# Moving five weight maxima and two patch normalisations between the steps of a fused vision-text layer

## The chip, the cores and the metric

The kernel runs on one core of a Trainium2 chip, as one program that holds the whole layer. The metric is the device time of one execution in microseconds. Three executions of the kernel before took 753.91, 754.61 and 766.34 us; the median is 754.61.

## The reference

64 images of 3 x 96 x 96 are cut into 36 patches of 768 numbers each. The patches are normalised, projected to 256 numbers, normalised again; a class token is put ahead and 32 text tokens behind, which gives 64 sequences of 69 tokens. Then come attention with 16 heads and rotary positions, and a layer of 8 experts, two for each token.

```python
patches = x.reshape(b, C, h, P, w, P).transpose(0, 2, 4, 3, 5, 1).reshape(b, h * w, P * P * C)
z = _layernorm(patches, ln1_g, ln1_b)
z = jnp.einsum('bnp,pe->bne', z, W_proj) + b_proj
z = _layernorm(z, ln2_g, ln2_b)
z = jnp.concatenate([cls, z], axis=1)
z = z + pos_emb
...
h = jnp.concatenate([h, txt], axis=1)
h = h + _L0_attn_ref(_layernorm(h, axis=-1), wq, wk, wv)
h = h + _L0_ffn_ref(_layernorm(h, axis=-1), moe_router, moe_w13, moe_w2)
```

## The kernel before

**Tiles.** The 2,304 patches make 18 patch tiles of 128 rows (n = 0 to 17), the 4,416 tokens make 35 token tiles (g = 0 to 34), and attention runs over 64 sequences (b). The work up to the experts is written as steps t from -12 (START) on. Each engine has a function `step(t)` that lists, under conditions on t, what the engine does in that step, and runs it for t = -12, -11 and so on. So the order on each engine is written out by hand, and engines meet only through semaphores; an engine that waits holds everything behind it in its own order. Steps aren't synchronised: engines can be some steps apart.

**Patch tiles.** Tiles 0 to 5 (EARLY) have their projection at the steps -10 to -5. One step later VectorE takes the statistics of z (`st2`, `mv2`) and PoolE (GpSimd) makes `rs2` and `off2`; two steps later ScalarE normalises z into `zout` (L1328) and PoolE multiplies by the gain and adds the positions (L819, L821); three steps later SyncE (SP) stores zout to the DRAM tensor `h_rows`, in four or five pieces (L637). `off2` and `rs2` have one buffer: PoolE makes those of tile n only when tile n - 1 is normalised (`zn_ready`). zout has two: ScalarE normalises tile n only when tile n - 2 is stored. Tiles from 6 on have their projection at the steps 4, 8, 13, 17 and so on.

**Token tiles.** SP loads a tile of tokens back as `h` (L613), VectorE takes its statistics (L1161, L1164), PoolE makes `off3`, ScalarE writes `xn` (L1367), PE turns it (L1460), ScalarE rounds it to fp16 as `fx_hi` (L1289), VectorE takes the rest as `fx_lo` (L1138), PE projects q and k (L1467), VectorE multiplies by the rotary table (`rot`, L1147), adds up k (L1153) and PoolE q (L784), PE turns both, and ScalarE saves `qT`, `kE`, `kO`. These take one step each: loads at first[g] - 6 and projection at first[g] - 2, for g = 0, 1, 2 and so on at the steps -2, -1, 1, 3, 5, 7, 9, 10, 12 and 14 (PJ). The other steps from 0 to 14 have no projection.

**Attention.** For sequence b, at step b PE makes the scores (L1607) in the PSUM tensor `quad`, and VectorE reduces them to row maxima (`nm_src`, L1101). At step b + 2 PE makes the scores again, turned, with the maxima taken off (L1671, L1675), again in quad, and ScalarE takes the exponentials (`probs`, L1383), for which the next scores in quad wait; at b + 3 PE weighs the values (L1575). So in each step scores, reduction, second scores and exponentials follow each other.

**Weight maxima.** The expert weights are later kept in fp16 halves under one common scale, which is found from their largest absolute value. For that SP loads them in 24 parts of 128 x 1024 (512 KB, L671) into a ring of three buffers `w_part`, and VectorE reduces each part to one column of `largest` (L1207). Part n is reduced at step -9 + n, one a step, to step 14, and its load is issued two steps before. The reduction stands near the end of VectorE's step: behind the statistics, and ahead of the next step's reduction of scores. At step 15 VectorE takes the maximum over all parts; the weights themselves are split from step 17 on.

## Time and profile before

| | |
|---|---|
| median of three runs | 754.61 us |
| the profiled execution | 758.35 us |
| its span, first to last instruction | 756.6 us |
| PE busy | 695.0 us (92%) |
| DVE (VectorE) busy | 549.4 us (73%) |
| POOL (GpSimd) busy | 456.1 us (60%) |
| ACT (ScalarE) busy | 403.6 us (53%) |
| mean granted TensorE clock | 0.951 |

The span is what one profiled execution took from its first to its last instruction. A busy share is an average over stages that have different limits. The page cuts the span into 40 slices of 18.9 us; the row of the granted clock (in tenths of full speed) shows where PE was given less:

```profile
PE   7857999999999999998888999999999999999994
DVE  3778887888888888897994457888756666566662
PEclk9977999999999999996995899999999999999999
```

The steps that the change touches run from about 30 to 142 us, in the slices 2 to 8. The experts begin at about 417 us.

### The profile page before, as it was taken

To read this page: it belongs to the slowest core of one execution; us is meant where nothing else is said; L and a number is where in the kernel's file an instruction comes from. 1 tells how busy PE (TensorE), PEld (TensorE's weight loads), DVE (VectorE), ACT (ScalarE), POOL (GpSimd) and SP (SyncE) were. 2 spreads that over 40 slices of the span, in tenths; PEclk is the share of its full clock that TensorE was granted. 3 is DMA by queue.
4 is the path that set the end of the run, shared out by engine and by line. 5 is a ranking of instruction groups with operands and counts; after the bars stand their busy time and mean duration, and the time that the engine had idled before them with its cause. 6 is when DMAs were issued, how large, how long until landed. Compare 5 with 4: busy or idle time off the path is not lost. (4 is left out here: it accounts for less than half of the span.)

```text
span 756.6 us, 27578 instructions
## 1 busy us (share of the span) xinstructions
PE 695.0 (92%) x9680; PEld 479.2 (63%) x9680; DVE 549.4 (73%) x1171; ACT 403.6 (53%) x893; POOL 456.1 (60%) x634
## 2 busy tenths in 40 slices
PE   7857999999999999998888999999999999999994
PEld 6724666767677776766667565556666666656663
DVE  3778887888888888897994457888756666566662
ACT  3334666677788778775765443333444434444341
POOL 5573644556576665645655367778666666666654
PEclk9977999999999999996995899999999999999999
DMA  8578666455545555553532377876878687777764
GB/s 296 183 212 288 206 197 219 128 154 169 167 138 176 152 176 141 169 155 110 139 113 83 96 121 127 107 122 114 128 128 134 121 140 124 131 135 127 134 113 77
DMA packets 145434, 112.52 MB, mean 149 GB/s; under 512 B 93545, under 2 KB 126073, under 8 KB 145240
## 3 DMA queue, kind: packets, MB, share of 16 engines
q1 hardware_dynamic: 129927, 86.75, 43.7%
q0 software_dynamic: 15376, 24.01, 19.1%
q8 instruction: 85, 1.39, 0.8%
q14 instruction: 46, 0.37, 0.2%
HBM read 58.95 MB, written 24.90 MB: 111 GB/s over the span
## 5 line engine op out<-in xcount | busy, mean ns | idle before, releaser
L425 POOL DMA_INDIRECT out<-qk,token_of x76 | 124.7, 1641 | 88.6 <-DVE small L513 47.5
L526 PE MATMUL quad<-w_hi,fx_hi 128*128 x304 | 116.2, 382 | 0.5 <-ACT fx_hi L453 0.5
L526 PE MATMUL quad<-w_lo,fx_hi 128*128 x304 | 116.2, 382 | 0.0
L526 PE MATMUL quad<-w_hi,fx_lo 128*128 x304 | 116.2, 382 | 0.0
L526 PE MATMUL bank<-w_hi,v 128*128 x608 | 112.0, 273 | 2.7 <-DMA v<-kO 2.3
L1383 ACT ACTIVATE probs<-quad 69x1104 f32<-69x1104 f32 x64 | 69.6, 1088 | 60.0 <-PE quad L1675 59.9
L1101 DVE TENSOR_REDUCE nm_src<-quad 69x16 f32<-69x1104 f32 x64 | 82.8, 1294 | 25.6 <-PE quad L1607 25.5
L490 DVE SCALAR_TENSOR_TENSOR probs<-quad,up_scale,vb 128x512 f32<-128x512 f32 x76 | 56.8, 748 | 52.1 <-PE quad L526 51.4
L402 POOL DMA_INDIRECT wc<-xn_rows,token_of x72 | 73.6, 1023 | 23.9 <-issue 19.6
L461 ACT ACTIVATE vb<-quad,unscale 128x512 f32<-128x512 f32 x76 | 52.3, 688 | 59.0 <-PE quad L526 58.9
L526 PE MATMUL bank<-w_lo,v 128*128 x304 | 82.9, 273 | 0.0
L526 PEld LDWEIGHTS bank<-w_hi,v 128*128 128x128 f16 x608 | 59.6, 98 | 18.3 <-issue 4.7
L736 POOL TENSOR_TENSOR rs<-ve,eps_pow 128x1 f32<-128x1 f32 (+1 forms) x106 | 62.3, 588 | 8.8
L784 POOL TENSOR_TENSOR qk<-rot 128x256 f32<-128x256 f32 (+1 forms) x35 | 34.0, 970 | 52.8 <-DVE rot L1147 52.8
L735 POOL TENSOR_SCALAR ve<-mv 128x1 f32<-128x1 f32 (+1 forms) x106 | 29.9, 282 | 57.7 <-DVE mv L1164 24.2
L776 POOL TENSOR_TENSOR h<-hb,att 128x256 f32<-128x256 f32 (+1 forms) x35 | 35.3, 1007 | 42.7 <-issue 30.7
L469 ACT ACTIVATE kE<-probs 128x512 f16<-128x512 f32 x38 | 24.0, 631 | 63.5 <-DVE probs L490 63.5
L469 ACT ACTIVATE kO<-probs 128x512 f16<-128x512 f32 x38 | 23.9, 630 | 63.0 <-DVE probs L490 63.0
L1671 PE MATMUL quad<-qT,kE 32*69 32x69 f32 x1024 | 46.8, 253 | 10.2 <-DVE nm_src L1101 9.9
L1467 PE MATMUL bank<-wqkv_hi,fx_hi 128*128 128x512 f16 (+2 forms) x140 | 49.8, 356 | 6.2 <-DVE fx_lo L1138 3.5
L526 PEld LDWEIGHTS quad<-w_hi,fx_lo 128*128 128x128 f16 x304 | 29.9, 98 | 35.8 <-issue 1.0
L1675 PE MATMUL quad<-nm,sel 32*69 32x69 bf16 x1024 | 51.6, 197 | 0.0
(273 smaller groups left out, 1768.3 us busy)
## 6 DMA issues: line engine op xcount, KB each, us to landing
w_lo<-in_experts_w SPq DMA_DIRECT2D x24, 512.0 KB, 6.3
w_raw<-in_experts_w SPq DMA_DIRECT2D x48, 256.0 KB, 4.2
xt<-in_patches SPq DMA_DIRECT2D x18, 384.0 KB, 6.0
h<-h_rows SPq DMA_DIRECT2D x34, 128.0 KB, 5.4
hb<-h_rows SPq DMA_DIRECT2D x34, 128.0 KB, 4.8
out<-h SPq DMA_DIRECT2D x34, 128.0 KB, 4.6
xn_rows<-xn SPq DMA_DIRECT2D x34, 128.0 KB
vb<-v SPq DMA_DIRECT2D x30, 138.0 KB
```

What stands on the lines that cost most here:

```text
L402: nc.gpsimd.indirect_dma_start(xg[n % DEPTH], None, reach(xn_rows, n), bass.IndirectOffsetOnAxis(token_of[:, n:n + 1], 0)).then_inc(gather ...
L425: nc.gpsimd.indirect_dma_start(reach(out, n), bass.IndirectOffsetOnAxis(token_of[:, n:n + 1], 0), y[q], None, compute_op=ALU.add).then_inc ...
L461: nc.scalar.activation(silu[q], quad[:, 2 * q, :], ACT.Silu, scale=unscale[:, 1:2]).then_inc(d["silu_ready"], 1)
L469: nc.scalar.activation(hid_parts[q][:, 0, :], hid[q], ACT.Copy).then_inc(d["hid_hi_ready"], 1)
L490: nc.vector.scalar_tensor_tensor(out=hid[q], in0=quad[:, 2 * q + 1, :], scalar=up_scale[:, :], in1=silu[q], op0=ALU.mult, op1=ALU.mult).th ...
L526: last = nc.tensor.matmul(dst, x[:, k, :], w[:, bass.ds(col + k * (2 * width if width == HIDDEN else width), width)], start=(k == 0 and m ...
L736: nc.gpsimd.tensor_tensor(rs, ve, eps_pow[0:rs.shape[0], :], ALU.pow).then_inc(signal, 1)
L1101: nc.vector.tensor_reduce(nm_src[b % 2][:, :].rearrange("p (g j) -> p g j", g=4)[:, :, 0:4], quad[0:SEQ, :, 0:4 * SEQ].rearrange("p g (j k ...
L1383: nc.scalar.activation(probs[b % 2][0:SEQ, :, :], quad[0:SEQ, :, 0:4 * SEQ], ACT.Exp, scale=HEAD_DIM ** -0.5).then_inc(s["probs_ready"], 1)
L1467: to = nc.tensor.matmul(dst, x[g % 2][:, k, 0:r], w[:, k, cols], start=(k == 0 and m == 0), stop=(k == KD - 1 and m == 2))
L1671: nc.tensor.matmul(quad[0:SEQ, g, j * SEQ:(j + 1) * SEQ], (kE, kO)[odd][band, c, at:at + SEQ], qT[band, c, at:at + SEQ], start=True, stop= ...
L1675: to = nc.tensor.matmul(quad[0:SEQ, g, j * SEQ:(j + 1) * SEQ], sel[band, j, :], nm[b % 2][band, :], start=False, stop=True)
```

## The change

The table of steps at which a part is reduced, so far one a step from -9 to 14, becomes a written list, `PART_STEPS`. The steps -6, -4, -1, 0 and 1 no longer have a part, and the steps 4, 6, 8, 11 and 13, none of which has a projection, have two. The load of a part is issued two steps ahead of its reduction, or, where its buffer comes free later than that, one step behind the reduction of the part three places before. And the patch tiles 4 and 5 (`LATE_NORM`; the fifth and the sixth) are normalised three steps behind their projection, not two: at -3 and -2 on ScalarE and PoolE, and their stores on SP come at -2 and -1. The semaphores and what they count stay as they are.

```diff
-PART_FROM = 3
+PART_STEPS = [-9, -8, -7, -5, -3, -2, *range(2, 15), 4, 6, 8, 11, 13]
+LATE_NORM = (4, 5)
...
-                part_step = {START + PART_FROM + n: n for n in range(PARTS)}
-                SCALE_STEP = START + PART_FROM + PARTS
+                part_step, part_load, part_at = {}, {}, sorted(PART_STEPS)
+                for n, k in enumerate(part_at):
+                    part_step.setdefault(k, []).append(n)
+                    part_load.setdefault(max(k - 2, part_at[n - PART_BUFS] + 1 if n >= PART_BUFS else k - 2), []).append(n)
+                SCALE_STEP = part_at[-1] + 1
+                normed = {mm_step[n] + (3 if n in LATE_NORM else 2): n for n in range(NT)}
...
-                            behind = t in HL and t - 3 in ZM and last_patch_tile[HL[t]] >= ZM[t - 3]
+                            behind = t in HL and t - 1 in normed and last_patch_tile[HL[t]] >= normed[t - 1]
...
-                            if t - 3 in ZM:
-                                n = ZM[t - 3]
+                            if t - 1 in normed:
+                                n = normed[t - 1]
...
-                            if t + 2 in part_step:
-                                n = part_step[t + 2]
+                            for n in part_load.get(t, ()):
...
-                            if t - 2 in ZM:
-                                n = ZM[t - 2]
+                            if t in normed:
+                                n = normed[t]
...
-                            if t in part_step:
-                                n = part_step[t]
+                            for n in part_step.get(t, ()):
```

The pieces with `t - 2 in ZM` stand twice, on PoolE and on ScalarE. Line numbers of the changed kernel are 5 or 6 higher from the planner on.

On ScalarE, from step -4 (xn of token tile 0) to step -1 (qT), before:

```order
L1367 ACTIVATE xn<-h,off,rs 128x256
L1328 ACTIVATE zout<-z,off,rs 128x256
L1289 ACTIVATE fx_hi<-bank 128x256
L1367 ACTIVATE xn<-h,off,rs 128x256
L1328 ACTIVATE zout<-z,off,rs 128x256
L1289 ACTIVATE fx_hi<-bank 128x256
L1289 ACTIVATE v<-bank,unscale 128x16x16
L1289 ACTIVATE qT<-bank 128x2x128
```

And now:

```order
L1372 ACTIVATE xn<-h,off,rs 128x256
L1294 ACTIVATE fx_hi<-bank 128x256
L1372 ACTIVATE xn<-h,off,rs 128x256
L1333 ACTIVATE zout<-z,off,rs 128x256
L1294 ACTIVATE fx_hi<-bank 128x256
L1294 ACTIVATE v<-bank,unscale 128x16x16
L1333 ACTIVATE zout<-z,off,rs 128x256
L1294 ACTIVATE qT<-bank 128x2x128
```

The first zout (patch tile 4) went behind fx_hi of token tile 0 and xn of token tile 1, the second (patch tile 5) behind fx_hi of tile 1 and v of tile 0.

On PoolE, at the steps -4 (the last off) to -1 (the second qk), before:

```order
L740 TENSOR_SCALAR off<-mv,rs 128x1
L819 TENSOR_TENSOR zout<-zout,gain 128x256
L821 TENSOR_TENSOR zout<-zout,shift 128x256
L819 TENSOR_TENSOR zout<-zout,gain 128x256
L821 TENSOR_TENSOR zout<-zout,shift 128x256
L784 TENSOR_TENSOR qk<-rot 128x256
L735 TENSOR_SCALAR ve<-mv 128x1
L736 TENSOR_TENSOR rs<-ve,eps_pow 128x1
L740 TENSOR_SCALAR off<-mv,rs 128x1
L784 TENSOR_TENSOR qk<-rot 128x256
```

And now:

```order
L746 TENSOR_SCALAR off<-mv,rs 128x1
L825 TENSOR_TENSOR zout<-zout,gain 128x256
L827 TENSOR_TENSOR zout<-zout,shift 128x256
L790 TENSOR_TENSOR qk<-rot 128x256
L741 TENSOR_SCALAR ve<-mv 128x1
L742 TENSOR_TENSOR rs<-ve,eps_pow 128x1
L746 TENSOR_SCALAR off<-mv,rs 128x1
L825 TENSOR_TENSOR zout<-zout,gain 128x256
L827 TENSOR_TENSOR zout<-zout,shift 128x256
L790 TENSOR_TENSOR qk<-rot 128x256
```

The pair of patch tile 5 went behind the addition of q of token tile 0 and the small chain of token tile 2.

On VectorE, from k of token tile 1 at step -1 to the score reduction of step 2, before:

```order
L1153 TENSOR_TENSOR qk<-rot 128x256
L1207 TENSOR_REDUCE largest<-w_lo 128x1
L1101 TENSOR_REDUCE nm_src<-quad 69x4x4
L1138 TENSOR_TENSOR fx_lo<-bank,fx_hi 128x256
L1161 BN_STATS st<-h 128x6
L1164 BN_AGGR mv<-st 128x2
L1207 TENSOR_REDUCE largest<-w_lo 128x1
L1101 TENSOR_REDUCE nm_src<-quad 69x4x4
L1147 TENSOR_TENSOR rot<-bank,rope_sb 128x1024
L1153 TENSOR_TENSOR qk<-rot 128x256
L1207 TENSOR_REDUCE largest<-w_lo 128x1
L1101 TENSOR_REDUCE nm_src<-quad 69x4x4
```

And now:

```order
L1159 TENSOR_TENSOR qk<-rot 128x256
L1107 TENSOR_REDUCE nm_src<-quad 69x4x4
L1144 TENSOR_TENSOR fx_lo<-bank,fx_hi 128x256
L1167 BN_STATS st<-h 128x6
L1170 BN_AGGR mv<-st 128x2
L1107 TENSOR_REDUCE nm_src<-quad 69x4x4
L1153 TENSOR_TENSOR rot<-bank,rope_sb 128x1024
L1159 TENSOR_TENSOR qk<-rot 128x256
L1107 TENSOR_REDUCE nm_src<-quad 69x4x4
```

The maxima ahead of the score reductions of steps 0, 1 and 2 are gone (they stood at the steps -1, 0 and 1). At step 4 and in the same way at 6, 8, 11 and 13 the row of the maximum now reads `x2`, in its old place.

## Rows read from the trace of the kernel before

**Rows 1.** The page: busy time, share of the span and instructions of each engine.

```profile
PE 695.0 (92%) x9680; PEld 479.2 (63%) x9680; DVE 549.4 (73%) x1171; ACT 403.6 (53%) x893; POOL 456.1 (60%) x634
```

**Rows 2.** Windows: busy us (count) PE, PEld, DVE, ACT, POOL; PEclk, DMA, GB/s.

```profile
60.00:80.00 20.00, 17.58 (x292) 11.38 (x293) 16.82 (x26) 9.37 (x25) 7.84 (x16) 0.74 0.76 251
80.00:150.00 70.00, 64.52 (x1442) 47.25 (x1442) 58.01 (x104) 44.54 (x109) 37.23 (x78) 0.95 0.61 188
```

**Rows 3.** Timeline, steps -4 and -3: start us, us, engine, line, operation, idle before.

```profile
43.47 0.66 PE L1460 MATMUL bank<-idt,xn 128*128 128x128 f32 x2 [3.67 <-ACT xn L1367]
...
44.74 0.60 ACT L1328 ACTIVATE zout<-z,off,rs 128x256 f32<-128x256 f32 x1 [1.41 <-DMA h_rows<-zout]
...
45.05 1.19 DVE L1207 TENSOR_REDUCE largest<-w_lo 128x1 f32<-128x1024 f32 x1
45.24 0.36 ACT L1289 ACTIVATE fx_hi<-bank 128x256 f16<-128x256 f32 x1
...
46.16 0.41 DVE L1138 TENSOR_TENSOR fx_lo<-bank,fx_hi 128x256 f16<-128x256 f32 x1
...
46.72 0.59 PE L1467 MATMUL bank<-wqkv_hi,fx_hi 128*128 128x512 f16 x1 [2.59 <-DVE fx_lo L1138]
...
46.86 0.60 ACT L1367 ACTIVATE xn<-h,off,rs 128x256 f32<-128x256 f32 x1 [1.26 <-POOL off L740]
46.91 0.22 POOL L735 TENSOR_SCALAR ve<-mv 128x1 f32<-128x1 f32 x1
...
48.91 0.73 POOL L821 TENSOR_TENSOR zout<-zout,shift 128x256 f32<-128x256 f32 x1
```

**Rows 4.** Timeline, steps -2 to 1.

```profile
51.95 0.96 POOL L784 TENSOR_TENSOR qk<-rot 128x256 f32<-128x256 f32 x1 [0.82 <-DVE rot L1147]
...
57.35 0.96 POOL L784 TENSOR_TENSOR qk<-rot 128x256 f32<-128x256 f32 x1 [3.11 <-DVE rot L1147]
57.64 1.21 DVE L1207 TENSOR_REDUCE largest<-w_lo 128x1 f32<-128x1024 f32 x1
...
58.77 1.29 DVE L1101 TENSOR_REDUCE nm_src<-quad 69x16 f32<-69x1104 f32 x1
...
60.31 0.23 PE L1607 MATMUL quad<-kE,qT 32*69 32x69 bf16 x4 [1.30 <-ACT kO L1289]
```

**Rows 5.** Timeline, steps 1 to 3.

```profile
64.99 1.21 DVE L1207 TENSOR_REDUCE largest<-w_lo 128x1 f32<-128x1024 f32 x1
...
66.12 1.29 DVE L1101 TENSOR_REDUCE nm_src<-quad 69x16 f32<-69x1104 f32 x1
...
67.47 0.52 PE L1671 MATMUL quad<-qT,kE 32*69 32x69 f32 x8 [1.10 <-DVE nm_src L1101]
...
69.00 0.43 DVE L1161 BATCH_NORM_STATS2 st<-h 128x6 f32<-128x256 f32 x1 [1.26 <-DMA h<-h_rows]
```

**Rows 6.** Timeline of DVE (one row of PE), steps 4 to 14.

```profile
81.41 0.48 DVE L1090 SCALAR_TENSOR_TENSOR z<-bank,rs,bias 128x256 f32<-128x256 f32 x1 [0.54 <-PE bank L1681]
82.52 1.30 DVE L1101 TENSOR_REDUCE nm_src<-quad 69x16 f32<-69x1104 f32 x1 [0.62 <-PE quad L1607]
...
92.45 1.30 DVE L1101 TENSOR_REDUCE nm_src<-quad 69x16 f32<-69x1104 f32 x1 [0.89 <-PE quad L1607]
...
103.89 0.48 DVE L1090 SCALAR_TENSOR_TENSOR z<-bank,rs,bias 128x256 f32<-128x256 f32 x1 [0.55 <-PE bank L1681]
105.40 1.30 DVE L1101 TENSOR_REDUCE nm_src<-quad 69x16 f32<-69x1104 f32 x1 [1.02 <-PE quad L1607]
...
120.08 0.32 PE L1575 MATMUL bank<-probs,vb 69*32 69x69 f32 x8 [1.64 <-issue]
...
121.51 1.30 DVE L1101 TENSOR_REDUCE nm_src<-quad 69x16 f32<-69x1104 f32 x1 [1.75 <-PE quad L1607]
...
133.22 0.48 DVE L1090 SCALAR_TENSOR_TENSOR z<-bank,rs,bias 128x256 f32<-128x256 f32 x1 [0.21 <-PE bank L1681]
134.34 1.30 DVE L1101 TENSOR_REDUCE nm_src<-quad 69x16 f32<-69x1104 f32 x1 [0.63 <-PE quad L1607]
```

## Predicting the time

> **What bounds the kernel now.** I read the page first: the span is 756.6 us, PE is busy 695.0 us of it, and no other engine comes near [rows 1]. That share hides what matters here. The windows view shows the granted clock. In the stretch from 60 to 80 us it averages 0.74, from 80 to 150 us it averages 0.95, and VectorE is busy 16.82 of 20 us in the first [rows 2]. The clock has two levels, 1.2 and 2.4 GHz (0.50 and 1.00), so 0.74 means that (1 - 0.74) / 0.5 = 52% of those 20 us, 10.4 us, ran at half speed. So in the first steps of the attention loop PE is often a waiting engine, slow once it gets going. Then I read the timeline of all engines from 43 to 71 us and the VectorE timeline on to 135 us.
>
> At steps -4 and -3 the first projection starts late. PE has turned token tile 0 from 43.47 (its record is 0.66 long), but ScalarE is held in the normalisation of patch tile 4 (44.74, after 1.41 us of waiting for the stores that free its buffer) and evacuates fx_hi only at 45.24. VectorE runs a maximum at 45.05 and makes fx_lo at 46.16; the projection begins at 46.72 [rows 3]. At steps -1 and 0 the maximum at 57.64 stands ahead of the score reduction at 58.77; the next scores start at 60.31 and name ScalarE's kO as what came last [rows 4]. At steps 1 and 2 the maximum at 64.99 stands ahead of the reduction at 66.12, and PE's second score pass (L1671) waits 1.10 us for that reduction and starts at 67.47 [rows 5]. Behind 142 us nothing that the change touches is left, and the chain runs in order through the same instructions; what is gained or lost there I carry to the end one for one.
>
> **The change, part by part.** No instruction is added or taken away: 24 loads of 512 KB and 24 maxima stay. A maximum costs VectorE 1.10 to 1.13 us from its start to the next start (45.05 to 46.16, 64.99 to 66.12) [rows 3, 5]; I use 1.1.
>
> *Step -6.* Its maximum goes. Behind it the next work is the statistics of h tile 0, which waits for a load anyway, and then PoolE work; I take 0, with 0 and 1.1 as bounds.
>
> *Step -4 and the later normalisation of tile 4.* ScalarE can take fx_hi when PE's turn ends, 43.47 + 0.66 = 44.13, instead of 45.24. It is then done by 44.5, and VectorE, without the maximum at 45.05, takes fx_lo at 45.05 instead of 46.16: 1.1 us. Both edits are needed: with the maximum gone alone fx_lo would wait for fx_hi until 45.6 (0.55 gained), with the normalisation moved alone the maximum would hold it (0 gained). The projection begins at 45.6. What the move puts at risk is PoolE: at step -4 it computes the offset of tile 5 only once tile 4 is normalised, and that now stands in ScalarE's step -3, behind xn of tile 1 (46.86 to 47.46). ScalarE ends it at 48.06; PoolE then has to do what it does now from 46.91 to 48.91 + 0.73, 2.7 us, and with a start-up of 0.3 comes to the addition of q at about 51.05, where it stood at 51.95 [rows 3, 4]. The rotation that it needs would be there at about 50.8, so of 1.1 us 0.9 survives. The second zout pair (tile 5) moves behind that addition, into a wait of PoolE of 3.1 us ahead of the next one [rows 4]: 0. The stores of tiles 4 and 5 come a step later too, five DMA issues of some 2 us in all on SP's queue at step -1, ahead of the first two loads of vb and of h tile 4; vb is wanted three steps later. I count 0 and keep this as a rival. Term: 0.9 (bounds 0 and 1.1).
>
> *Steps -1 and 0.* Without the maximum at 57.64 the reduction at 58.77 starts 1.1 us sooner on top of the 0.9. But the next scores, at 60.31, came when ScalarE's kO of tile 1 was there, and that hangs on the projection, which moved by 0.9 only [rows 4]. So these two maxima were hidden behind PE and ScalarE: 0 (bounds 0 and 2.2).
>
> *Step 1.* The maximum at 64.99 goes, the reduction starts 1.1 us sooner, and PE's pass at 67.47 and the exponentials and scores behind it with it: PE waited 1.10 us for just this [rows 5]. Term: 1.1 (bounds 0 and 1.1).
>
> *The doubled steps 4, 6, 8, 11 and 13.* The second maximum takes 1.1 us of VectorE and costs only what it exceeds the idle time between the first one and the next score reduction [rows 6]. Step 4: VectorE is idle 0.54 ahead of z (81.41) and 0.62 ahead of the reduction at 82.52, 1.16 in all: 0. Step 6: 0.89 ahead of 92.45: 0.2. Step 8: 0.55 ahead of z and 1.02 ahead of 105.40: 0. Step 11: 1.75 ahead of 121.51: 0; most of that cover is a hole of 1.64 us in PE's own stream (120.08, "issue"), without which the step would cost the full 1.0. Step 13: 0.21 ahead of z and 0.63 ahead of 134.34: 0.3. Together 0.5 (bounds 0 and 5.5).
>
> *The sum*: 0.9 + 1.1 - 0.5 = 1.5 us gained. The profiled execution took 758.35 us (span 756.6) and would take 756.85; the median of the runs is 754.61, so I forecast 754.6 - 1.5 = **753.1 us**. The profiled execution lies 3.7 us over the median, more than twice the effect, so a change of this size is near the least that the runs can show.
>
> **The clock.** The row of 60 to 80 us says that 10.4 us ran at half speed, and PE was busy 17.58 us of that stretch, so dense but slow [rows 2]. If the waits that go leave PE denser and a third of that time comes back at full speed, 10.4 / 3 / 2 = 1.7 us more are gained; at the utmost 5.2. In the other direction, the stretch from 80 to 150 us has 0.05 / 0.5 = 10% or 7.0 us at half speed; another 3.5 us of it would cost 1.7. The Trainium skill, "TensorE: Matmul & The Clock Gate", section "HAM oscillation — how this bites in real kernels", says that bursts of matmuls broken by waits fall back to the slow clock again and again. By that rule the gain would be 3.2 us rather than 1.5, at the price just worked out. It cuts both ways: by the same rule the five doubled steps, where PE now runs at full clock, might lose it. The trace agrees so far as the slow stretches all lie behind waits of PE, but it cannot say where they fall after the change.
>
> **The rivals.**
> - *The doubled maxima are not covered (slower).* VectorE is the bound of the steps without a projection as soon as the idle time behind a maximum is under 1.1 us. Rows 6 show 1.16, 0.89, 1.57, 1.75 and 0.84; four of the five are near that point [rows 6], and a step that PE reaches sooner (a warmer clock, no hole at 120.08) loses its cover. Price: 5 x 1.1 - 2.0 = 3.5 us, 758.1 us. Against it: all five waits are for PE, whose program is the same, and it has nothing that would bring it sooner by itself.
> - *Nothing arrives.* The projections at half clock and the waits for h bound the steps, and what is won at -4 and 1 is only waited for later: VectorE waits 1.26 us for h at 69.00 already [rows 5]. 754.6 us.
> - *The clock comes back as well*: 1.5 + 1.7 to 1.5 + 3.4, so 751.4 to 749.7, say 750.5 us. For it: slow stretches just behind the waits that go; and three loads of 512 KB fewer in steps -3 to -1 also bring h sooner.
> - *The clock is lost later*: 753.1 + 1.7 = 754.8 us.
> - *SP's queue*: the late stores delay h of tile 4, whose wait of 1.26 grows by as much again: 753.1 + 1.3 = 754.4 us [rows 5].
>
> **How the numbers follow.** Forecast (751.6 to 754.2): 0.45. Clock back: 0.20. Nothing arrives: 0.14. Maxima not covered: 0.12. Clock lost: 0.05. SP's queue: 0.04. The range that leaves out no more than 2 in 10 goes from 748.8, where the sum and the full 3.4 us of clock come together and a little of the rest of the 5.2, to 757.5, where nearly all five maxima are exposed; the likeliest case alone is 751.6 to 754.2. Faster or slower by over 2% is 15 us, about what a measurement of this kernel can tell from no change, and no case reaches it: faster 0.01, same 0.97, slower 0.02.
>
> **What would show it.** In the profile after: fx_lo of tile 0 near 45.1 and the projection near 45.6; q added near 51; the first reduction near 56.8 with no maximum ahead of it; the scores of step 1 still waiting for kO, at 59.4; PE's pass of step 2 near 65.4 with no wait for VectorE. Then the reductions of steps 5, 7, 9, 12 and 14 1.5 to 2 us sooner than now, which says that the doubled maxima were free; if this lead shrinks by 1 us at one of them, that one was not. A first projection that is not sooner, or PoolE's addition of q no sooner than 51.95, would show the term of step -4 wrong; a mean clock in 58 to 76 us unlike 0.74 would show the rival.

## The result, and the profile after

Six runs of the changed kernel took 766.04 to 775.34 us, median 769.79; six runs of the kernel before beside them had a median of 757.12. The ratio is 1.017, with a 95% interval of 1.013 to 1.022: the change makes the kernel some 13 us slower. Ratios here and below leave out executions that fell in a slower state, whatever the kernel (766.34 us once here, 1316.53 and 1651.04 us once each below); the medians hold them. I had forecast 753.1 us, 1.5 less than the median of three runs before (754.61), and at most 757.5. Direction and range were wrong.

The page of the profiled execution (775.34 us, the longest of the six), instructions by engine and three rows of the 40 slices (19.3 us each here):

```profile
PE 699.0 (90%) x9680; PEld 482.4 (62%) x9680; DVE 551.1 (71%) x1171; ACT 403.5 (52%) x893; POOL 455.9 (59%) x634
...
PE   7864998799999999998888999999999999999994
...
DVE  4765888678978878987996466788755665666562
...
PEclk9968889899999999997895799999999999999997
```

The counts are those of [rows 1] and the busy times within 4 us of them, while the span grew by 17.0 (756.6 to 773.6). So the new time is waiting. The windows, with the columns of [rows 2]:

```profile
58.00:64.00 6.00, 3.76 (x51) 2.26 (x51) 5.13 (x8) 3.19 (x8) 2.05 (x5) 1.00 0.54 151
64.00:76.00 12.00, 4.01 (x78) 2.42 (x78) 3.75 (x6) 3.17 (x7) 2.48 (x6) 0.81 0.70 230
76.00:80.00 4.00, 3.84 (x86) 3.23 (x87) 3.90 (x7) 1.61 (x3) 2.06 (x5) 0.50 0.75 238
80.00:150.00 70.00, 60.13 (x1258) 43.30 (x1259) 56.19 (x89) 38.12 (x92) 30.09 (x62) 0.89 0.68 215
```

From 64 to 76 us PE works 4.01 us of 12, and no other engine more than 3.75; behind it PE runs at half clock for 4 us (0.50). To place the losses I compared the starts of the 64 score reductions (`nm_src`), one for each step, in the timelines of both kernels. After minus before, in us:

| step | 0 | 1 | 2 | 3 | 5 | 8 | 12 | 13 | 14 | 16 | 40 | 63 |
|---|---|---|---|---|---|---|---|---|---|---|---|---|
| changed kernel | -1.4 | -1.7 | -2.8 | +4.0 | +4.6 | +5.8 | +6.8 | +5.8 | +10.5 | +12.8 | +12.9 | +13.8 |

A lead of 2.8 us is built up to step 2; step 3 loses 6.8, and the steps 14 to 16 lose 7.0. The remaining 3.2 us of the span come behind the last reduction. These sizes are those of one execution, and the longest of six: the places of the losses are firmer than their sizes.

**The lead** has the forecast's sign, but not its terms. Timeline from step -4 on; each line is a start, a duration, an engine, a line, an operation, and the idle time before it:

```profile
44.08 0.38 ACT L1294 ACTIVATE fx_hi<-bank 128x256 f16<-128x256 f32 x1 [0.59 <-PE bank L1465]
44.49 0.42 DVE L1144 TENSOR_TENSOR fx_lo<-bank,fx_hi 128x256 f16<-128x256 f32 x1
...
45.06 0.58 PE L1472 MATMUL bank<-wqkv_hi,fx_hi 128*128 128x512 f16 x1 [1.02 <-DVE fx_lo L1144]
...
50.98 0.91 POOL L790 TENSOR_TENSOR qk<-rot 128x256 f32<-128x256 f32 x1
...
57.41 1.30 DVE L1107 TENSOR_REDUCE nm_src<-quad 69x16 f32<-69x1104 f32 x1
...
59.92 0.23 PE L1612 MATMUL quad<-kE,qT 32*69 32x69 bf16 x4 [1.29 <-ACT kO L1294]
...
60.30 1.30 DVE L1107 TENSOR_REDUCE nm_src<-quad 69x16 f32<-69x1104 f32 x1 [0.71 <-PE quad L1612]
61.70 1.22 DVE L1153 TENSOR_TENSOR rot<-bank,rope_sb 128x1024 f32<-128x1024 f32 x1
...
63.30 1.30 DVE L1107 TENSOR_REDUCE nm_src<-quad 69x16 f32<-69x1104 f32 x1
...
64.65 0.36 PE L1676 MATMUL quad<-qT,kE 32*69 32x69 f32 x8
```

And before, between the scores of step 1 (60.31 [rows 4]) and their reduction:

```profile
60.86 1.19 DVE L1207 TENSOR_REDUCE largest<-w_lo 128x1 f32<-128x1024 f32 x1
61.96 1.29 DVE L1101 TENSOR_REDUCE nm_src<-quad 69x16 f32<-69x1104 f32 x1
```

PoolE's q comes 0.97 us sooner, the scores of step 1 only 0.39 us (PE's turn of q and k took 1.11 us instead of 0.66). Their reduction comes 1.66 us sooner, since the maximum of step 0 no longer stands ahead of it, and that of step 2 comes 2.82 us sooner without the maximum of step 1. So the lead is about 0.4 + 1.3 + 1.1 us, and nearly half of it is the maximum of step 0.

**The first loss** stands right behind it:

```profile
73.14 0.43 DVE L1167 BATCH_NORM_STATS2 st<-h 128x6 f32<-128x256 f32 x1 [8.22 <-DMA h<-h_rows]
...
76.16 0.52 PE L1676 MATMUL quad<-qT,kE 32*69 32x69 f32 x8 [7.28 <-DVE nm_src L1107]
```

VectorE waits 8.22 us for token tile 4, where it waited 1.26 [rows 5]. The statistics stand ahead of the reduction of step 3 on VectorE, and PE waits 7.28 us for that. SP's own queue in that stretch (here the duration is that of the issue alone):

```profile
55.56 1.87 SPq L644 DMA_DIRECT2D h_rows<-zout  x5
57.48 1.54 SPq L663 DMA_DIRECT2D vb<-v  x2
59.06 0.78 SPq L665 DMA_DIRECT2D vb<-v  x1
59.89 0.48 SPq L677 DMA_DIRECT2D w_lo<-in_experts_w  x1
60.95 0.34 SPq L620 DMA_DIRECT2D h<-h_rows  x1
```

The load was issued at 60.95, only 0.9 us later than before (60.01), but took 12.2 us to land (60.95 to 73.14) instead of 9.0 (60.01 to 69.00). So it isn't SP's queue that is slow, but what the load meets once it is issued. The five late stores now stand directly ahead of the first loads of `vb`.

**The second loss**, VectorE and SP at the steps 11 to 14:

```profile
126.97 1.22 DVE L1212 TENSOR_REDUCE largest<-w_lo 128x1 f32<-128x1024 f32 x1 [0.97 <-DMA w_lo<-in_experts_w]
...
133.34 1.97 SPq L677 DMA_DIRECT2D w_lo<-in_experts_w  x2
...
141.77 1.22 DVE L1212 TENSOR_REDUCE largest<-w_lo 128x1 f32<-128x1024 f32 x1 [4.04 <-DMA w_lo<-in_experts_w]
143.34 1.22 DVE L1212 TENSOR_REDUCE largest<-w_lo 128x1 f32<-128x1024 f32 x1 [0.35 <-DMA w_lo<-in_experts_w]
```

Both parts of step 13 are issued in SP's step 12, one step ahead and not two: with three buffers their places in the ring come free only with the two reductions of step 11. The same holds for the steps 6 and 8, and by the rule of the diff single parts lose a step as well (those of 5, 7, 9, 10, 12 and 14): 14 of the 24 loads go out one step ahead. VectorE then waits 4.04 + 0.35 us for the two of step 13. The other 2.6 us up to step 16 have no wait for a part beside them; PE's granted clock from 145 to 150 us is 0.51, where it was 1.00 before.

### The profile page after: what moved, and what is told of

It reads as the page before. It is cut to its first block and busy times, and to the rows that moved or that the text cites. A ratio compares the mean times of both kernels' runs of the same rounds, so it can differ in the third digit from the quotient of the medians.

```text
span 773.6 us, 27578 instructions
## 1 busy us (share of the span) xinstructions
PE 699.0 (90%) x9680; PEld 482.4 (62%) x9680; DVE 551.1 (71%) x1171; ACT 403.5 (52%) x893; POOL 455.9 (59%) x634
## 5 line engine op out<-in xcount | busy, mean ns | idle before, releaser
L497 DVE SCALAR_TENSOR_TENSOR probs<-quad,up_scale,vb 128x512 f32<-128x512 f32 x76 | 56.8, 748 | 54.8 <-PE quad L533 54.3
L741 POOL TENSOR_SCALAR ve<-mv 128x1 f32<-128x1 f32 (+1 forms) x106 | 28.2, 266 | 66.4 <-DVE mv L1170 31.8
L1676 PEld LDWEIGHTS quad<-qT,kE 32*69 32x69 f32 x1024 | 30.3, 148 | 40.2 <-DVE nm_src L1107 27.0
```

The source lines that it names most:

```text
L497: nc.vector.scalar_tensor_tensor(out=hid[q], in0=quad[:, 2 * q + 1, :], scalar=up_scale[:, :], in1=silu[q], op0=ALU.mult, op1=ALU.mult).th ...
L1676: nc.tensor.matmul(quad[0:SEQ, g, j * SEQ:(j + 1) * SEQ], (kE, kO)[odd][band, c, at:at + SEQ], qT[band, c, at:at + SEQ], start=True, stop= ...
```

## The experiments

Three theories to begin with. *S*: the later normalisation, by its stores, delays h at step 3. *L*: the loads of doubled parts, with one step of lead, are late. *D*: the doubled maxima themselves cost VectorE's time. All ratios below are to runs of the kernel before on the same chip, in three rounds unless said otherwise, with 95% intervals. Its median was 759.83 us beside the first four kernels, and 758.64 (order, even cut, table with four buffers), 756.52 (odd cut to the kernel before with the cut), 759.01 and 759.23 us beside the later groups. The ratios aren't quotients of these medians. The two differ most in the group at 756.52, where the executions of before lie in two heaps (754 to 759 and 760 to 765 us): the quotients for its four kernels are 1.018, 1.014, 1.008 and 1.004 where the ratios given below are 1.0096, 1.0097, 1.0033 and 0.9981. No reading below rests on that difference. "Lead" is the start of a score reduction against the profiled execution of before, minus being sooner. A single lead is rough: in two kernels that differ from before up to step 1 in nothing or only in the pieces of vb (*doubled maxima* and *before, cut* below), the reduction of step 1 starts 0.6 and 2.3 us later than there.

### Each part of the change alone

The later normalisation alone, and the table alone:

```diff
-PART_STEPS = [-9, -8, -7, -5, -3, -2, *range(2, 15), 4, 6, 8, 11, 13]
+PART_STEPS = list(range(-9, 15))
```

> The parts stand as before (one a step, -9 to 14); only the normalisations of patch tiles 4 and 5 come one step later. Theory S (the late stores of tile 5 push the first vb load on SP from 55.05 to 57.48, and its rows and those of the second vb share few DMA engines with the load of h tile 4, whose wait at VectorE grows from 1.26 to 8.2 us): most of the loss at steps 2 to 3 appears here, 755 + 4 to 6 us, and VectorE waits over 5 us for h. Theory P (the part loads that now bunch at steps 0 to 2 beside the text load delay h): no wait over 2 us for h, time within 2 us of before.

```diff
-LATE_NORM = (4, 5)
+LATE_NORM = ()
```

> Only the table of parts is changed, the patch tiles 4 and 5 are normalised as before. Theory S: the wait for h tile 4 stays near 1 to 3 us, but the waits of VectorE for weight parts in the doubled steps (5.6 us in the changed kernel, 4.0 of it at step 13) stay: before + 5 to 8 us. Theory P: the wait for h is 6 to 9 us as in the changed kernel: before + 10 to 13 us.

Measured: the normalisation alone 763.61 us, 1.0063 [1.0022, 1.0104]; it has a wait of 6.95 us for h, no lead at all at step 2 (+0.7) and +6.2 at step 3. The table alone 767.23 us, 1.0146 [1.0079, 1.0212]; its lead at step 2 is the whole 2.8, step 3 keeps 1.9, but the waits for parts sum to 8.5 us over the whole profile and the lead turns to +5.9 by step 16. So S and L both hold. I had expected 5 to 8 us for the table alone; the ratio says 11, the medians say 7. And the later normalisation, without which fx_lo was to wait until 45.6, brought nothing: in the table alone ScalarE normalises patch tile 4 already at 43.98 (44.74 before), with no wait for a store, and fx_lo starts at 44.88.

### Four buffers, and the text earlier

```diff
-PART_BUFS = 3
+PART_BUFS = 4
```

> The changed kernel with a ring of four part buffers, so that both loads of a doubled step go out two steps ahead. Theory L (a doubled step costs because its loads have one step of lead in place of two, 5 to 6 us against 7 to 10 us to landing): the waits for parts fall from 5.6 us to under 1 and the lead lost at steps 12 to 15 (5.8 to 12.0 us) is mostly won back, changed kernel - 5 to 7 us. Theory D (VectorE's own 1.1 us each is what costs): no more than 1 us changes.

A second idea for the first loss (theory T in the expectation; its theory P is that the part loads themselves delay h) was that the text (768 KB, issued by PoolE at 63.91) meets h. This kernel issues it three steps sooner, the rest as changed:

```diff
-TXT_STEP = [None, 1, 9]
+TXT_STEP = [None, -2, 9]
```

> The changed kernel with PoolE's second text load (768 KB, 24 pieces of 32 KB) issued at step -2 in place of 1, about 8 us sooner, when the DMA engines stand nearly idle. Theory T (the large pieces of the text are what hold h tile 4 back): the wait of 8.2 us for h falls under 3 us, changed kernel - 5 to 6 us. Theory S or P: the wait falls by 1 to 2 us at most.

With four buffers: 766.78 us, 1.0129 [1.0079, 1.0178], by the ratios 3 us better than the changed kernel's 1.0172, with intervals that overlap; I had expected 5 to 7. From step 12 (+6.0) to step 16 (+6.4) only 0.4 us is lost, where the changed kernel lost 6.0, with the five maxima doubled all the same:

```profile
123.41 2.31 DVE L1212 TENSOR_REDUCE largest<-w_lo 128x1 f32<-128x1024 f32 x2
127.49 1.30 DVE L1107 TENSOR_REDUCE nm_src<-quad 69x16 f32<-69x1104 f32 x1 [1.77 <-PE quad L1612]
...
137.91 2.31 DVE L1212 TENSOR_REDUCE largest<-w_lo 128x1 f32<-128x1024 f32 x2
140.53 1.29 DVE L1107 TENSOR_REDUCE nm_src<-quad 69x16 f32<-69x1104 f32 x1
```

So the second loss is the loads' short lead. With four buffers only one load for each of the steps 6, 8 and 13 keeps one step of lead, and the other 21 have two, which is enough here. How much is lost from step 12 to 16 varies: 1.9 to 6.1 us in the five kernels with five moved parts and three buffers, 0.4, 0.4 and 0.8 in three with four buffers, but 3.2 in the fourth (the changed kernel with cut and four buffers, below), which waits 1.23 us for a part of step 13.

The text earlier: 769.25 us, 1.0157 [1.0112, 1.0202]; the wait for h is 5.47 instead of 8.22. That can't be credited to the text: with four buffers, where neither the text nor any load ahead of h was moved, it is 4.49. Between steps 2 and 3 the changed kernel loses 6.8 us, the normalisation alone 5.5, the text version 4.1, four buffers 3.1: the price of the first loss is 3 to 7 us, and the profiled execution of the changed kernel shows its upper end.

### What h meets: the loads of vb

`vb` is loaded from SBUF to SBUF, the 69 rows of a sequence in one piece or in two (59 + 10, 49 + 20). The Trainium skill, "DMA: Bandwidth & Descriptors", section "Why a DMA increments its semaphore by 16 and not by 1", says that a DMA is spread over the largest number of engines up to 16 that divides the slowest dimension of both its sides. By that rule 69 rows use 3 engines, 59 rows one and 49 rows 7, and a load of 128 rows, spread over all 16, would queue on those few. No row of a profile view tells which engine moved a packet; so I tested it by its effect. First the order, then the shape:

```diff
-                            if t - 1 in normed:
+                            if t - 1 in normed and t != -1:
...
+                            if t == -1:
+                                store_z(t)
```

(The stores of patch tile 5 now go behind the loads of vb.)

> The changed kernel, only that at step -1 SP issues the five stores of patch tile 5 behind the loads of vb (in the changed kernel they stand ahead of them and push them to where they meet two parts and h tile 4). Order theory (the late stores move the vb loads into the path of h): the wait for h ahead of its statistics falls from 8.22 us to under 3, the score reduction of step 3 comes at least 4 us sooner than in the changed kernel, and the whole gains 4 to 6 us on it, about 764 us where before stands near 758. Volume theory (parts, h, text and xt are too much for the engines whatever the order): the wait stays over 6 us and the time stays near 769.

For the shape, the normalisation alone (1.0063) with the pieces of the sequences 0 to 3 cut at a multiple of 16:

```diff
+                    cut = [(lo, lo + (hi - lo) // 16 * 16, hi) for lo, hi in runs]
+                    return [x for lo, mid, hi in cut for x in ((lo, mid), (mid, hi)) if x[0] < x[1]]
```

> The kernel before with the later normalisation alone (as in the earlier run of that edit), and the loads of vb for the sequences 0 to 3 cut into pieces of 64 + 5, 48 + 11 + 10, 64 + 5 and 48 + 1 + 16 + 4 rows instead of 69, 59 + 10, 69 and 49 + 20. Theory of few engines (a load whose rows have no common divisor with 16 is moved by few of the 16 DMA engines, and h queues behind it there): the wait for h at step 3 falls from 6.95 us to under 2, and the whole from 1.006 of before to 1.000 (3 to 5 us gained on the uncut one). Rival (all engines are equally loaded): the wait stays between 6 and 8 us, the time 1.005 to 1.008, since more DMA issues stand on SP's queue.

And its control, the same number of issues and bytes with other cuts:

```diff
-                    cut = [(lo, lo + (hi - lo) // 16 * 16, hi) for lo, hi in runs]
+                    cut = [(lo, lo + {69: 61, 59: 47, 49: 47, 20: 19, 10: 0}[hi - lo], hi) for lo, hi in runs]
```

> The control of the cut. The same edit of the normalisation and the same number of DMA issues for vb, but the cuts fall at rows that don't divide by 16: 61 + 8, 47 + 12 + 10, 61 + 8 and 47 + 2 + 19 + 1 rows instead of 64 + 5, 48 + 11 + 10, 64 + 5 and 48 + 1 + 16 + 4. Theory of few engines: the wait for h at step 3 is back at 5 us or more (6.95 uncut, 0.62 with the even cut), h takes over 8 us from its issue to its landing where the even cut had 3.8 us, and the time is 1.005 to 1.010 of before. Rival (it was the number or the later place of the issues that helped: with the even cut h goes out at 65.4 us instead of 61): the wait stays under 2 us and the time at 1.000.

The order: 767.08 us, 1.0141 [1.0082, 1.0200]. The wait for h fell from 8.22 to 2.66 us and step 3 leads by 1.8, as the order theory had it; but the parts at the steps 4 to 13 were late all the more (waits of 7.8 us in all). The time hardly moved: I had expected 4 to 6 us less than the changed kernel, and the ratios differ by 0.3%, with intervals that overlap.

The shape, first the even cut, then the odd one; the DMA view of the stretch from 58 to 70 us (count, size, median from issue to landing) and VectorE's wait for h:

```profile
w_lo<-in_experts_w SPq DMA_DIRECT2D x3, 512.0 KB, 4.8
h<-h_rows SPq DMA_DIRECT2D x1, 128.0 KB, 3.8
...
69.22 0.43 DVE L1178 BATCH_NORM_STATS2 st<-h 128x6 f32<-128x256 f32 x1 [0.62 <-DMA h<-h_rows]
```

```profile
w_lo<-in_experts_w SPq DMA_DIRECT2D x2, 512.0 KB, 9.9
h<-h_rows SPq DMA_DIRECT2D x1, 128.0 KB, 11.8
...
75.18 0.43 DVE L1178 BATCH_NORM_STATS2 st<-h 128x6 f32<-128x256 f32 x1 [5.12 <-DMA h<-h_rows]
...
90.99 0.43 DVE L1178 BATCH_NORM_STATS2 st<-h 128x6 f32<-128x256 f32 x1 [5.80 <-DMA h<-h_rows]
```

Even: 758.60 us, 0.9998 [0.9964, 1.0033]. Odd: 770.06 us, 1.0096 [1.0049, 1.0143]. The slowest of the ten executions with the even cut (763.71 us) is faster than the fastest of the six with the odd one (767.38, on another chip). The same bytes in the same number of pieces, and h lands in 3.8 us or in 11.8; 512 KB take 4.8 or 9.9. The number of issues is ruled out by that. Nor is it their place: with the even cut h was issued 2 us later than with the odd one (65.39 and 63.34) and landed 6 us sooner (69.22 and 75.18). So the first loss is what h meets behind vb, and the shape of the vb pieces decides it. That it meets them on few engines is an inference, which the trace supports: with the odd cut the 16 DMA engines are busy only 0.23 on average from 68 to 74 us (77 GB/s), while h, issued at 63.34, still hasn't landed. The rule of the page predicts which cut is which.

### The remedies together

The part table with four buffers and the old normalisation, without and with the even cut; then the changed kernel with the cut, with cut and four buffers, and the kernel before with the cut alone.

> The part table of the change, the normalisation as before, and four buffers for the parts instead of three, so that the doubled steps' loads go out two steps ahead again. Both losses should then be absent: the lead of 2.8 us at the score reduction of step 2 is kept to the end, the waits for parts at the late steps are under 1 us in sum, the whole 1 to 3 us faster than before (0.996 to 0.999). If the loads that pile up at the steps 2 to 5 delay h of tiles 4 and 5 here too (the part table alone had 3.8 us of h waits), the lead is gone by step 5 and the time is 1.000 to 1.004 of before. If the doubled maxima themselves cost VectorE (rival of the prediction, 3.5 us), the loss shows as reductions falling back at the steps 5, 7, 9, 12 and 14 with no DMA wait beside them.

> As the kernel with the part table and four buffers, and the vb loads of the sequences 0 to 3 cut so that most of their rows divide by 16. Theory of few engines: h no longer waits at the steps 3 to 5, and the whole is 2 to 4 us faster than without the cut (0.993 to 0.996 of before). Rival: no difference to the uncut one over 1 us.

> The changed kernel whole, with the vb loads of the sequences 0 to 3 cut evenly (64 + 5 and so on). If the two losses are separate, the first (6.8 us at step 3) goes and the second (7 us at the steps 13 to 16, loads of the doubled parts only one step ahead) stays: reductions 2 to 3 us sooner than before from step 3 to 12, later by 3 to 5 from step 16 on, the whole 1.003 to 1.008 of before. If the second loss too comes from the vb loads, the time is at or under that of before.

> The changed kernel with both remedies: the even cut and four buffers for the parts. Both losses gone, the lead of 2.8 us or more at step 2 is kept to the end: 0.994 to 0.998 of before. If it stays at 1.000 or over, a third cost is left, to be seen in the reductions after step 4.

> The kernel before with the even cut alone. In it h waited only 1.26 us at step 3, so the cut can give little: 0.997 to 1.000 of before, and with it the gain of the versions with both edits can be told from the gain of the cut itself. If it gives 3 us or more (0.996 or less), most of what the cut gave in the other versions has nothing to do with the change.

| kernel | us | ratio | step 2 | 3 | 5 | 12 | 16 |
|---|---|---|---|---|---|---|---|
| table, 4 buffers | 763.45 | 1.0074 [1.0033, 1.0116] | -1.2 | -1.1 | +2.2 | +2.6 | +3.4 |
| the same, cut | 760.17 | 1.0031 [0.9999, 1.0062] | -4.5 | -5.2 | -5.2 | -3.6 | -3.3 |
| changed, cut | 767.38 | 1.0097 [1.0044, 1.0150] | -3.1 | -3.2 | +0.9 | +5.7 | +11.8 |
| changed, cut, 4 buffers | 762.76 | 1.0033 [0.9986, 1.0081] | -5.0 | -4.7 | -0.9 | +2.2 | +5.4 |
| before, cut | 759.35 | 0.9981 [0.9937, 1.0025] | +2.0 | +2.0 | +2.0 | +1.4 | +1.4 |

(The profiled execution of the second row, 753.84 us, was the fastest of its ten, so its steps look better than its ratio.) With late stores the cut keeps the lead over step 3 (changed, cut; changed, cut, 4 buffers); without them it is kept there in any case (table, 4 buffers). The second loss stays where there are three buffers (changed, cut: +5.7 to +11.8). I had expected 0.994 to 0.998 of the changed kernel with both remedies and 0.993 to 0.996 of the table with both, 1.5 to 5 us faster than before. They aren't: no version that moves five parts is faster than before. Nor did the changed kernel with the cut keep its lead to step 12. Where a lead is lost again, it is between the steps 4 and 6, to another load that is late:

```profile
81.86 1.22 DVE L1223 TENSOR_REDUCE largest<-w_lo 128x1 f32<-128x1024 f32 x1 [3.45 <-DMA w_lo<-in_experts_w]
```

(changed, cut) and, in the changed kernel with cut and four buffers,

```profile
78.41 0.43 DVE L1178 BATCH_NORM_STATS2 st<-h 128x6 f32<-128x256 f32 x1 [5.43 <-DMA h<-h_rows]
```

In both one stretch of four vb issues had held SP for 5 to 6 us, where four took 2.5 us in the table's version with the cut. But the normalisation alone with the even cut had such a stretch too (5.25 us) and no such loss, so what delays these loads stays open.

### VectorE's share alone

Two kernels move no load at all. One doubles the maxima at the five late steps (into a column that nothing reads). One shortens the five early ones to 16 of 1024 columns, and so leaves most of five parts out of the weights' maximum:

```diff
+                                if t in (4, 6, 8, 11, 13):
+                                    nc.vector.tensor_reduce(twice[:, t:t + 1], w_part[n % PART_BUFS], AX.X, ALU.max,
+                                                            apply_absolute_value=True)
```

> The kernel before, with the maximum of the part done twice at the steps 4, 6, 8, 11 and 13 (the second one into a column that nothing reads) and no load moved: 29 maxima instead of 24, VectorE's price of the doubling by itself. By the idle times of the rows of before (the prediction's term) it costs 0.5 us, and the score reductions of the steps 5, 7, 9, 12 and 14 fall behind by at most 0.3 each: 1.000 to 1.001 of before. If the maxima aren't covered, they fall behind by up to 1.1 each and the whole by 3.5 to 5.5: 1.005 to 1.007.

```diff
+                                part = w_part[n % PART_BUFS][:, 0:16] if t in (-6, -4, -1, 0, 1) else w_part[n % PART_BUFS]
```

> The kernel before, with the maxima of the steps -6, -4, -1, 0 and 1 over 16 of their 1024 columns (this leaves most of five parts out of the maximum of the weights), all loads at their place: VectorE's part of the lead. If the lead of 2.8 us at the reduction of step 2 is VectorE's time, it appears here in full (2.2 to 3), and with no load moved it is kept to the end: 0.996 to 0.998 of before. The prediction's terms with the normalisation as before would be 0.55 + 1.1 = 1.6 us. If the lead came from the loads that left the steps -8 to -1, it is under 1 us here.

Short maxima: 760.86 us, 0.9990 [0.9957, 1.0023]. The profile has the lead, 2.35 us at step 2, and then:

```profile
63.77 1.29 DVE L1107 TENSOR_REDUCE nm_src<-quad 69x16 f32<-69x1104 f32 x1
...
70.92 0.43 DVE L1167 BATCH_NORM_STATS2 st<-h 128x6 f32<-128x256 f32 x1 [5.52 <-DMA h<-h_rows]
```

The lead is VectorE's own time, and in this execution it is gone at step 3, where h decides. h was issued at 59.99, as before, and landed 1.9 us later than there. Five maxima that cost next to nothing make the kernel no faster by more than this measurement resolves; its interval reaches down to 0.9957, so a gain of up to 3 us, and with it the 1.6 of the expectation, isn't excluded by the times.

Doubled maxima: 762.85 us, 1.0049 [1.0011, 1.0087], some 3.7 us. Its profiled execution (759.33, near the fastest of the ten) doesn't show that loss: the reductions go from +0.3 at step 2 to -0.7 at step 14, and the rows between the steps 4 and 5 show 1.2 us lost, which later steps take back:

```profile
80.40 0.43 DVE L1168 BATCH_NORM_STATS2 st<-h 128x6 f32<-128x256 f32 x1 [1.29 <-DMA h<-h_rows]
...
80.96 1.19 DVE L1214 TENSOR_REDUCE twice<-w_lo 128x1 f32<-128x1024 f32 x1
82.07 1.21 DVE L1216 TENSOR_REDUCE largest<-w_lo 128x1 f32<-128x1024 f32 x1
83.19 0.47 DVE L1097 SCALAR_TENSOR_TENSOR z<-bank,rs,bias 128x256 f32<-128x256 f32 x1
83.58 1.29 DVE L1108 TENSOR_REDUCE nm_src<-quad 69x16 f32<-69x1104 f32 x1
```

Before, VectorE had 1.16 us of idle time there [rows 6] and no wait for h. The second maximum (1.11 us from start to start) would just fit into it; with the 1.29 us for h ahead of it, it doesn't. So by the runs D has a part as well; its size stays open between 0.8 and 6.6 us, and where it falls isn't shown.

### Moving two parts only

Only the parts of the steps -4 and 1, to the steps 8 and 11, which had the most idle time [rows 6]; four buffers; normalisation as before; with and without the even cut:

```diff
+PART_STEPS = [-9, -8, -7, -6, -5, -3, -2, -1, 0, *range(2, 15), 8, 11]
```

> Only the parts of the steps -4 and 1 leave, for the steps 8 and 11 (the two with the most idle time ahead of the next reduction, 1.57 and 1.75 us), normalisation as before, four buffers, and the even cut of the vb loads: 0.994 to 0.998 of before, faster than the kernel with five moved parts and the same remedies (1.0031). If the lead at step 2 is under 1.5 us, the maxima of -1 and 0 were needed for it; if it is lost between the steps 4 and 7 as in the others, the loads there are late whatever the table.

> The same table and four buffers without the cut of the vb loads: 1 to 3 us slower than with it, 0.997 to 1.001 of before, with a wait for h of 1 to 3 us at one of the steps 3 to 5.

> The kernel before with four buffers for the parts and the even cut of the vb loads, no part moved, normalisation as before. If the gain of the version with two moved parts (0.9951) is the moved maxima's, this one stays at 0.998 to 1.001 of before, and that version is 2 us or more faster than it in the same call. If the gain is the remedies' own, it is at 0.995 to 0.997 here too.

> The version with two moved parts, four buffers and the even cut once more, five rounds: 0.993 to 0.998 of before, interval under 1.000. At 0.999 or over the first comparison was luck.

With the cut 755.07 us, 0.9951 [0.9915, 0.9987]: faster than both kernels. Without it 757.50 us, 0.9970 [0.9935, 1.0005]. Repeated in five rounds: 757.02 us, 0.9957 [0.9924, 0.9989]; beside it the kernel before with four buffers and the cut, nothing moved: 756.64 us, 0.9980 [0.9951, 1.0010]. The gain on before holds in both groups, 0.4 to 0.5%. That the two moved parts have a share in it isn't shown: the two versions can't be told apart, and my expectation of 2 us between them failed. Nor did the two parts give a lead: the reduction of step 2 stands at +0.5, -0.1 and -1.2 us in the three profiles. Only the last piece of it, the maximum of step 1, is there each time: from step 1 to 2 they win 1.3, 1.3 and 1.4 us. By the sign named in the expectation (a lead under 1.5 us) the maxima of the steps -1 and 0 were needed for the lead, which fits the 1.3 us found for step 0. In the first one's profile behind 50 us only two waits for loads are left, of 0.62 and 0.60 us, and a doubled maximum is covered, with waits of 0.53 and 1.42 us for PE left ahead of the reductions behind it:

```profile
98.86 2.31 DVE L1223 TENSOR_REDUCE largest<-w_lo 128x1 f32<-128x1024 f32 x2
101.09 0.47 DVE L1107 SCALAR_TENSOR_TENSOR z<-bank,rs,bias 128x256 f32<-128x256 f32 x1
102.09 1.30 DVE L1118 TENSOR_REDUCE nm_src<-quad 69x16 f32<-69x1104 f32 x1 [0.53 <-PE quad L1623]
...
115.27 2.31 DVE L1223 TENSOR_REDUCE largest<-w_lo 128x1 f32<-128x1024 f32 x2
119.00 1.30 DVE L1118 TENSOR_REDUCE nm_src<-quad 69x16 f32<-69x1104 f32 x1 [1.42 <-PE quad L1623]
```

## Why the prediction was wrong

- **Step -6**, counted as 0: not isolated by any run.
- **Step -4 and the later normalisation**, 0.9. The first places were right: fx_lo at 44.49 (45.1 foretold), the projection at 45.06 (45.6), PoolE's q at 50.98 (51.05). But of the 0.9 us only 0.39 reached the scores of step 1 (59.92, not 59.4). And "both edits are needed" failed: the table alone has all of the lead (-2.8 at step 2), the normalisation alone none. The second half of the change bought nothing.
- **Steps -1 and 0**, 0. For step -1 that holds: its reduction comes 1.36 us sooner (57.41; 56.8 foretold), and the scores of step 1 wait for kO all the same. For step 0 it failed: the argument showed that the *scores* of step 1 don't hang on these maxima, and left out that their reduction (61.96 before) stood behind the maximum of step 0. It is worth 1.3 us.
- **Step 1**, 1.1: right. PE's second pass starts at 64.65 (65.4 foretold) without its wait of 1.10 [rows 5]. All terms up to here gave 2.0 us, and 2.8 were measured: 0.4 + 1.3 + 1.1 in place of 0.9 + 0 + 1.1. That the sum came near is in part luck.
- **The late stores**, "I count 0", and the rival *SP's queue* at 1.3 us with a chance of 0.04: this is the step that failed first. The normalisation alone is at 1.0063 of before, some 5 us slower, and step 3 loses 6.8 us in the profiled execution (3.1 to 5.5 in the three other kernels with late stores and uncut vb). I priced the five issues on SP ("some 2 us"; 1.87 measured) and not what the transfers meet. The row for it was at hand: h waited 1.26 us [rows 5] for a load that took 9 us, where the median of all 34 loads of h is 5.4 on the page of before. What stretched that load to 1.7 times its median had no term, and its cost couldn't be bounded by doubling the wait.
- **"24 loads of 512 KB and 24 maxima stay"**: true of the count, and it hid the second failure. The diff puts loads of doubled steps one step behind the reduction three places before, in place of two ahead. I read it, told it in the part on the change and gave it no term. Part loads in the trace of before took 9.3 to 12.7 us when issued from 59 to 72 us, and 6 to 8 us from 80 us on; a step there is 5.7 us on average. So a wait of 1 to 2 us at a doubled step was to be had from the trace (an estimate). Price: 7.0 us at the reductions of the steps 14 to 16, of which 4.4 are waits for parts (6.0 counted from step 12, and 0.4 there with four buffers).
- **The doubled maxima**, 0.5, rival 3.5 at 0.12: the runs give 0.8 to 6.6 us when they are doubled alone. In the changed kernel late loads stand beside most of the pairs and hide what the pairs cost. The rival's price may be the better one, but no profile here shows it.
- **Nothing arrives**, 0.14: for the gain the traces show this, though the times alone don't prove it (0.9990, down to 0.9957). VectorE's lead of 2.35 us, taken alone, turned into a longer wait for h at step 3. I named that row and still let the 1.5 us pass it. h was due at 69.00 and VectorE was waiting for it from 67.74: whatever came sooner on VectorE could only lengthen that wait while the load didn't move.
- **The clock.** From 58 to 64 us it is 1.00 (0.72 before), and the sign that I had named, the mean of 58 to 76 us, is 0.87 (0.72 before). So the rival *clock back* has a part in the lead: at the matmul times of before (0.63 us each in place of 0.38), q and k of tile 2 would have taken from 60.19 to about 62.9, not to 61.7, where `rot` starts, so some 1.2 of the 2.8 us hang on the clock (an estimate from these rows; not tested). Later it went the other way: 76 to 80 is at 0.50 and 80 to 150 at 0.89 instead of 0.95. The clock fell behind the long waits, so *lost later* came true as a companion of the two losses: (0.95 - 0.89) / 0.5 x 70 = 8.4 us more at half speed, at most 4.2 us of time. None of the 6.8 us is this, since the reduction of step 3 (74.81) waited for h and VectorE, not for PE; how much of the other losses is, I didn't separate.

The sum as measured, in the one profiled execution: -2.8 (lead) + 6.8 (h at step 3) + 2.8 (steps 4 to 13 and 17 to 63) + 7.0 (parts at the steps 13 to 16) + 3.2 (experts) = 17.0 us of span between the two profiled executions; 12.7 between the medians.

## What to carry to other kernels

Before work is moved off a compute engine, look at the next wait for a DMA on the path: a gain ahead of it is lost there unless that load comes sooner too. When an edit moves loads or stores, give each a term of its own, with its lead (issue to use) against the slowest landing in that stretch, not against the median, and recount the lead where a ring of buffers decides when a load may go. Where a landing takes well over its median, look for small transfers with awkward row counts ahead of it, and try cutting them at a multiple of 16. Here that brought the later normalisation from 1.0063 to 0.9998 of before; on the kernel before itself it gave nothing that could be measured (0.9981, 0.9937 to 1.0025). And list what stands behind an instruction on its own engine: a maximum can be hidden for the next scores and still hold their reduction.

## What the hardware showed

- How an SBUF-to-SBUF load is split into pieces of rows matters to its neighbours: with pieces such as 64 + 5 rows a 128-KB load issued behind them landed in 3.8 us, with 61 + 8 and the like in 11.8, and the kernel was at 0.9998 and 1.0096 of before.
- Beside busy DMA engines issuing itself can be slow: in the changed kernel, with the DMA engines busy 1.00 from 64 to 68 us, a load of h that otherwise takes SP 0.34 us held it for 3.35 us, and with it all that stood behind on SP:

```profile
65.64 3.35 SPq L620 DMA_DIRECT2D h<-h_rows  x1
```
